# A graph layer and a mixture of experts in one kernel: logits from unnormalised tokens, and where the round's stores are awaited

## What is computed

```python
x = x + gnn(layernorm(x))          # 625 tokens x 512
x = x + ffn(layernorm(x))

# gnn: 16 relations' products H[r] = xn @ W_rel[r].T + b_rel[r], 10625 edges (both ways),
#      summed by target node, plus xn @ W_self.T + b_self, relu
# ffn: logits = xn @ router_w.T (16 experts), top 2, softmax over the two,
#      out = sum over the two experts of weight * (silu(xn @ gate) * (xn @ up)) @ down
#      gate, up: 512 x 1024, down: 1024 x 512 for each expert
```

## Time and profile before

| what | value |
|---|---|
| time, median of 3 runs | 737.27 us (736.48 to 740.19) |
| the profiled execution's own time | 733.35 us |
| its span, first to last instruction | 731.6 us |
| PE busy | 694.9 us |
| DVE busy | 625.8 us |
| ACT busy | 502.0 us |
| POOL busy | 309.9 us |

### The profile page before, as it was taken

The page is one execution under the profiler, slowest core; times in us unless marked ns, Lnnn a source line. Parts: engine busy times, 40 slices in busy tenths (PEclk is TensorE's granted clock), DMA queues, the critical chain, the costliest instruction groups (busy, mean ns, idle before and its releaser), DMA issues. The chain is left out here.

```text
span 731.6 us, 10688 instructions
## 1 busy us (share of the span) xinstructions
PE 694.9 (95%) x3210; PEld 542.9 (74%) x3210; DVE 625.8 (86%) x1289; ACT 502.0 (69%) x717; POOL 309.9 (42%) x279
## 2 busy tenths in 40 slices
PE   5899999999998999999997999999999999999993
PEld 4777766777676777777755788888888888888883
DVE  8889979998999677777775899999998999999990
ACT  3655476665675777777556498888877888888870
POOL 3000077851787677777771033332234333333201
PEclk9999999999999999999998899999999999999997
DMA  7347589884888889998767989999999999999932
GB/s 243 126 144 270 168 267 305 299 257 144 301 281 295 276 280 306 315 295 244 217 196 239 379 321 354 405 394 392 405 355 396 370 379 374 361 403 379 357 110 30
DMA packets 54436, 212.75 MB, mean 291 GB/s; under 512 B 9753, under 2 KB 10150, under 8 KB 39158
## 3 DMA queue, kind: packets, MB, share of 16 engines
q1 hardware_dynamic: 34998, 153.85, 55.9%
q0 software_dynamic: 19392, 58.35, 27.4%
HBM read 184.36 MB, written 27.80 MB: 290 GB/s over the span
## 5 line engine op out<-in xcount | busy, mean ns | idle before, releaser
L400 POOL DMA_INDIRECT rows_sb<-h_dram,row_of x190 | 212.5, 1119 | 165.3 <-DVE row_of L549 84.1
L559 DVE TENSOR_TENSOR rows_lo<-rows_sb,rows_hi 128x512 fp32r<-128x512 f32 x175 | 120.1, 686 | 43.5 <-ACT rows_hi L697 43.4
L830 PE MATMUL p_h<-g_hi_sb,xt_hi_whole 128*125 128x512 f32 x320 | 128.4, 401 | 0.3 <-DVE g_lo_sb L503 0.3
L831 PE MATMUL p_h<-g_lo_sb,xt_hi_whole 128*125 128x512 f32 x320 | 126.7, 396 | 0.0
L832 PE MATMUL p_h<-g_hi_sb,xt_lo_whole 128*125 128x512 f32 x320 | 126.5, 395 | 0.0
L697 ACT CAST rows_hi<-rows_sb 128x512 fp32r<-128x512 f32 x175 | 100.1, 619 | 25.5 <-DMA rows_sb<-h_dram,row_of 23.3
L682 ACT COPY h_whole<-p_h 125x512 f32<-125x512 f32 x80 | 46.9, 586 | 89.2 <-PE p_h L832 89.1
L1195 POOL DMA_INDIRECT tokens<-token_dram,rows_of_tokens x15 | 22.1, 1470 | 170.8 <-ACT rows_of_tokens L1484 131.5
L864 PE MATMUL p_sum<-rows_hi,seg_hot 128*125 128x512 f32 x175 | 73.6, 421 | 5.4 <-DVE rows_lo L559 4.5
L1248 DVE TENSOR_TENSOR u_lo_sb<-stage_up,u_hi_sb 128x2048 fp32r<-128x2048 f32 x34 | 76.4, 2288 | 1.0
L1248 DVE TENSOR_TENSOR d_lo_sb<-stage_down,d_hi_sb 128x2048 fp32r<-128x2048 f32 x32 | 71.8, 2286 | 3.0 <-ACT d_hi_sb L1469 2.9
(11 more groups left out here) (292 smaller groups left out, 1363.6 us busy)
## 6 DMA issues: line engine op xcount, KB each, us to landing
stage_up<-in_L_ffn_up_w SPq DMA_DIRECT2D x34, 1024.0 KB, 8.0
stage_gate<-in_L_ffn_gate_w SPq DMA_DIRECT2D x32, 1024.0 KB, 8.7
stage_down<-in_L_ffn_down_w SPq DMA_DIRECT2D x32, 1024.0 KB, 7.5
h_dram<-h_whole SPq DMA_DIRECT2D x80, 224.0 KB
stage_up<-in_L_gnn_W_rel SPq DMA_DIRECT2D x16, 1024.0 KB, 8.0
x_whole<-in_L_gnn_b_rel SPq DMA_DIRECT2D x16, 256.0 KB, 9.7
rows_sb<-h_dram,row_of POOLq DMA_INDIRECT x190, 5.1
h_dram<-h_whole SPq DMA_DIRECT2D x80, 26.0 KB
```

Source lines behind the costliest of these rows:

```text
L400: q.indirect_dma_start(rows_sb[:, b % ROWS], None, h_dram[0:1 + made(n) * TP], bass.IndirectOffsetOnAxis(ap=row_of[:, b:b + 1].bitcast(U32 ...
L559: v.tensor_tensor(rows_lo[:, b % PARTS], rows_sb[:, b % ROWS], rows_hi[:, b % PARTS].bitcast(F32), ALU.subtract).then_inc(part_lo, 1)
L830: m.matmul(o, xt_hi[:, dc, at], wt_hi_sb[:, 1 - j % 2, dc], start=(by_matmul and dc == 0), stop=False, skip_group_check=True)
L831: m.matmul(o, xt_hi[:, dc, at], wt_lo_sb[:, 1 - j % 2, dc], start=False, stop=False, skip_group_check=True)
```

## The change

- The router's weights are centred: at product 72 (ROUTER) four matmuls with an all-ones matrix sum `router_t` over the 512 features, and DVE subtracts the mean (`centre_router`, by product 73). The logits are then made of x2 instead of xn: PE's `turn` waits for x2 and not for the normalisation, and its logits are those of before times 1/rstd. The gap of the two best is multiplied by rstd before Exp.
- PE's turns and logits come one tile sooner in its list, and so do ACT's copies.
- The last tile is normalised, and split in parts, in the second block: ACT at its beginning, DVE's `last_low` between the two groups of one-hots.
- SP no longer waits for the up weights and the stores at the round's end. Those two semaphores are no longer cleared; whoever overwrites x2's memory or reads the up weights waits for them: SP before the loads of d (and in the next round before its first weights), POOL before its gathers, ACT before the high parts of u. The token rows' store waits for the last tile.
- In the second block `choose` is cut in `candidates` and the rest, and the early one-hots go ahead of most of it; x_low(0) goes ahead of `chosen` and of u's first low part. PE picks expert 1's first two tiles ahead of `turn_tokens(0)` and the rest behind it, ahead of the ranks, with one `keep_going` matmul in place of three. On ACT both picked_copy and x_high(0) go ahead of Exp and Silu.

```diff
@@ on_sync
+                sp.wait_ge(up_loaded, nth_round * 32 + 16)
+                sp.wait_ge(x2_stored, nth_round * (32 * T) + 16)
                 w_load(0)
...
                     sp.dma_start(out[t * TP + MAIN:(t + 1) * TP], x2[MAIN:TP, t]).then_inc(x2_stored, 16)
-                sp.wait_ge(up_loaded, 32)
-                sp.wait_ge(x2_stored, 32 * T)
@@ on_vector
+                def centre_router():
+                    dve.wait_ge(router_summed, 1)
+                    v.scalar_tensor_tensor(router_t[:], p_router.unsqueeze(1).to_broadcast([P, KC, NX]), -1 / D, router_t[:],
+                                           ALU.mult, ALU.add).then_inc(router_ready, 1)
...
+                    if i == ROUTER + 1:
+                        centre_router()
...
                     if t:
                         token_lows(t - 1)
-                token_lows(T - 1)
@@ on_scalar
                 for t in range(T):
-                    if t >= 2:
-                        x2_copy(t - 2)
-                    if t == T - 1:
+                    if t:
                         x2_copy(t - 1)
-                    root(t)
-                    normal2(t)
-                    high2(t)
                     if t == T - 1:
                         x2_copy(t)
+                    root(t)
+                    if t < T - 1:
+                        normal2(t)
+                        high2(t)
                     carry_out(t)
+                act.wait_ge(scale2_ready, T)
@@ on_tensor
                 def turn(t):
-                    pe.wait_ge(ln2_ready, t + 1)
+                    pe.wait_ge(x2_ready, t + 1)
...
-                        i = m.transpose(p_h[:, t % 2, dc * TP:(dc + 1) * TP], xn[:, t, dc * P:(dc + 1) * P], ident[0:TP, 0:TP])
+                        i = m.transpose(p_h[:, t % 2, dc * TP:(dc + 1) * TP], x2[:, t, dc * P:(dc + 1) * P], ident[0:TP, 0:TP])
...
+                    if i == ROUTER:
+                        pe.wait_ge(small_loaded, 16)
+                        pe.wait_ge(rows_ready, 2)
+                        for dc in range(KC):
+                            r = m.matmul(p_router, ones[:], router_t[:, dc], start=(dc == 0), stop=(dc == KC - 1))
+                        r.then_inc(router_summed, 1)
...
                 for t in range(T):
                     for k in range(last_in_tile):
                         last_message(last_span + t * last_in_tile + k)
+                    if t:
+                        turn(t - 1)
                     if t >= 2:
-                        turn(t - 2)
-                    if t >= 3:
-                        token_logits(t - 3)
-                turn(T - 2)
-                token_logits(T - 3)
+                        token_logits(t - 2)
+                turn(T - 1)
                 token_logits(T - 2)
-                turn(T - 1)
                 token_logits(T - 1)
@@ first block, SP
+                    sp.sem_inc(up_loaded, 16)
+                    sp.sem_inc(x2_stored, 16)
                     sp.dma_start(edge[:], edges).then_inc(edge_loaded, 16)
@@ second block, SP and POOL
                     load("g", 1, 0)
                     load("g", 1, 1)
+                    sp.wait_ge(last_hi_ready, 1)
...
+                    sp.wait_ge(x2_stored, sp.snap(rounds_of(sp), min_val=1, max_val=ROUNDS) * (32 * T) + 16)
                     load("d", 0, 0)
...
+                    pool.wait_ge(x2_stored, pool.snap(rounds_of(pool), min_val=1, max_val=ROUNDS) * (32 * T) + 16)
                     pool.wait_ge(ln2_stored, 32)
@@ second block, DVE
+                    def last_low():
+                        dve.wait_ge(last_hi_ready, 1)
+                        v.tensor_tensor(xn_lo[:, T - 1], xn[:, T - 1], xn_hi[:, T - 1].bitcast(F32), ALU.subtract).then_inc(last_lo_ready, 1)
...
                     def chosen():
-                        v.tensor_tensor(mask[:, 0:T], hot[:, 0], hot[:, 1], ALU.add).then_inc(mask_ready, 1)
-                        v.tensor_tensor(gap[:], best[:, 1], best[:, 0], ALU.subtract).then_inc(gap_ready, 1)
+                        link("dve", dve, v.tensor_tensor(gap[:], best[:, 1], best[:, 0], ALU.subtract))
+                        v.tensor_tensor(gap[:], gap[:], rstd[:], ALU.mult).then_inc(gap_ready, 1)
...
                     early_masks()
+                    candidates(0)
+                    early_places()
+                    early_hots(0)
+                    last_low()
+                    early_hots(1)
                     choose(0)
-                    early_hots()
+                    candidates(1)
                     choose(1)
+                    v.tensor_tensor(mask[:, 0:T], hot[:, 0], hot[:, 1], ALU.add).then_inc(mask_ready, 1)
+                    x_low(0)
                     chosen()
                     low("u", 0, 0)
-                    x_low(0)
                     places()
@@ second block, ACT
                     act.sem_inc(split_hi["g"], 2)
+                    t = T - 1
+                    s.activation(xn[:, t], x2[:, t], ACT.Identity, bias=shift[:, t:t + 1], scale=rstd[:, t:t + 1]).then_inc(last_ln_ready, 1)
+                    act.wait_ge(last_ln_ready, 1)
+                    s.copy(xn_hi[:, t], xn[:, t]).then_inc(last_hi_ready, 1)
+                    n = act.snap(rounds_of(act), min_val=1, max_val=ROUNDS)
+                    act.wait_ge(x2_stored, n * (32 * T) + 16)
+                    act.wait_ge(up_loaded, n * 32 + 16)
                     high("u", 0, 0)
                     high("u", 0, 1)
+                    picked_copy(0)
+                    x_high(0)
+                    picked_copy(1)
                     act.wait_ge(gap_ready, 1)
                     s.activation(gap[:], gap[:], ACT.Exp).then_inc(exp_ready, 1)
...
                     s.activation(idle[:], gap[:], ACT.Silu)
-                    picked_copy(0)
-                    x_high(0)
-                    picked_copy(1)
                     x_high(1)
@@ second block, PE
-                    keep_going(3)
-                    pick_tokens(0)
+                    keep_going(1)
+                    pick_tokens(0, range(T))
+                    pick_tokens(1, range(0, 2))
+                    turn_tokens(0)
+                    pick_tokens(1, range(2, T))
                     pe.wait_ge(mask_ready, 1)
...
-                    turn_tokens(0)
-                    pick_tokens(1)
                     pe.wait_ge(xt_lo_ready, 1)
```

More of the change, by code:

```diff
@@ L43 @@
 LAG, START, PACE = 3, 22, 3.0
-LAST_HOTS = 56
+LAST_HOTS, ROUTER = 56, 72
 LOW, BIASES = 32, 2 * R + 1
@@ L119, in build @@
         gathered = [sem(f"gathered{i}") for i in range(ROWS)]
+        up_loaded, x2_stored = sem("up_loaded"), sem("x2_stored")
         steps, pool_steps = sem("steps"), sem("pool_steps")
         edge_consts, route_consts, spare_cleared = sem("edge_consts"), sem("route_consts"), sem("spare_cleared")
-        small_loaded, gate_loaded, x2_stored = sem("small_loaded"), sem("gate_loaded"), sem("x2_stored")
+        small_loaded, gate_loaded = sem("small_loaded"), sem("gate_loaded")
+        router_summed, router_ready = sem("router_summed"), sem("router_ready")
         bias_hi, bias_ready, self_ready = sem("bias_hi"), sem("bias_ready"), sem("self_ready")
@@ L249, in build @@
             p_logits = p_list[0:TP, 0:T * NX].rearrange("p (t e) -> p t e", t=T)
+            p_router = p_list[:, 256:256 + NX]
             p_ranks = p_sum[:, 0:3]
@@ L304, in turned, with on_sync @@
                 return p_sum[:, 3 + t % 2, 0:KC * TP].rearrange("p (c n) -> p c n", c=KC)
-            def on_sync(sp):
+            def on_sync(sp, nth_round):
                 def w_load(j):
@@ L932, in on_tensor @@
                             self_product(t)
-                pe.wait_ge(small_loaded, 16)
+                pe.wait_ge(router_ready, 1)
                 pe.wait_ge(round_counted, 1)
@@ L992, in _ @@
                     def _(sp):
-                        on_sync(sp)
+                        on_sync(sp, nth_round)
                     @block.gpsimd
@@ L1288, in early_hots, with candidates @@
                         link("dve", dve, v.scalar_tensor_tensor(early_place[:], p_early.rearrange("p (t e) -> p t e", t=T), 1.0, early_mask[:], ALU.add, ALU.mult))
-                        for e in range(2):
-                            for t in range(T):
-                                i = v.tensor_scalar(early_hot[e][:, t], slot_iota[:], 1.0, early_place[:, t, e:e + 1], ALU.add, ALU.is_equal)
-                                i.then_inc(early_hot_ready, 1)
-                    def choose(c):
+                    def early_hots(e):
+                        for t in range(T):
+                            i = v.tensor_scalar(early_hot[e][:, t], slot_iota[:], 1.0, early_place[:, t, e:e + 1], ALU.add, ALU.is_equal)
+                            i.then_inc(early_hot_ready, 1)
+                    def last_low():
+                        dve.wait_ge(last_hi_ready, 1)
```

(12 more changed lines are left out.)

5 lines of the change are left out of this document (3 added, 2 removed).

## The result

The changed kernel took 734.8 us (median of 20 runs, 728.16 to 739.66), the kernel before 737.95 on the same chip (20 runs, 734.91 to 741.38). The ratio is 0.9953 with a 95% interval of 0.9934 to 0.9972, so 3.5 us were gained, between 2.1 and 4.9. Its profiled execution took 732.14 us, its span is 730.4.

What follows compares the result with a forecast made beforehand. PE, busy 95%, was taken as the bound, with SP's wait for stores setting the round's boundary. Terms -4.15 + 0.55 + 0.1 - 0.35 = -3.85 us took 737.27 to 733.4 us; range 732.0 to 736.5.

Steps and rivals of the forecast that it cites:

- round's end, x2 to B: Graph layer's end: without SP's wait for stores, DVE arrives last at 395.6, not SP at 399.74; block begins 4.15 us earlier.
- router, in the product loop: PE's product loop: four new 16-column matmuls cost 0.55 us after a gap takes some; bounds 0 and 0.95.
- SP at the start, to the first product: Round's start: two semaphore increments before SP's first load cost 0.1 us, between 0 and 0.2.
- second block to the gate product: Second block up to expert 1's gate product: of some 2.4 us PE wins by reordering, 0.35 us remain.
- The wait moved to ACT: Second block's begin: ACT waits 1.1 us for stores landing at 400.4, holding u's high parts and all of expert 0.
- rival of stores delayed by loads: Round's end: gate-weight loads share the DMA engines, stores land 1 to 2 us later; gain 1.8 to 2.8, chance 0.23.
- ACT's 407.6 decides, by a little: Before x_low(0): ACT's u parts end at 407.6, PE's picks at 407.4, so ACT sets x_low(0) at 409.56.
- the low level at the block's begin and a rise 5 us into it: PE's clock: low at the second block's begin, rising 5 us in; a rise 2 us later costs about 1 us.
- A stall of about 2 us shows: Before expert 1's gate product: PE ready at 422.3, product can start at 424.3 behind DVE's first g low part.
- The block does begin earlier: Opposing rival: round's end waits on something hidden behind SP, so no earlier block; 737.4 us, chance 0.04.
- +4.6 us: Round's end rival: stores land behind loads and token rows, ACT begins u at 409; 741.9 us, chance 0.06.
- If PE entered at 2.4 GHz: Second block's begin: clock high, DVE decides instead of PE or ACT, worth at most 0.9 us; more gain's chance 0.12.

Runs made afterwards that it cites:

- base: The changed kernel with the second block's wait thresholds for stores and up weights written as constants for one round; 735.27 us against 737.67 for before, 0.9961.
- second profile of before: The unchanged kernel before, profiled again beside three experiments; 736.63 us, x2 to turns 39.35 us against 38.75 in its first profile.
- loads behind: The base with the two loads of expert 1's gate weights put behind the wait for the stores; 764.89 us, 1.0004, on a chip where before takes 764.7.
- old order: The base with the second block's work in the order of before, the last tile still normalised in it; 734.84 us, 0.9966 of before.
- slots late, end filler: The base with expert 1's slots work behind its gate product, plus four wide matmuls behind the last logits at the round's end; 737.7 us, 0.9993 of before.
- slots late, split: The base with slots work behind expert 1's gate product, turn_tokens(2) amid down(0), x_low(2) behind expert 2's first g low part; 738.57 us, 0.9992.
- the slots late: The base with slot_hots, PE's slots matmuls and ACT's copies of them moved behind expert 1's gate product; 737.63 us, 1.0013 of before.
- both fillers: The base with seven matmuls without a reader ahead of expert 1's gate product and four behind the last tile's logits; 736.28 us, 0.9961 of before.

## Why the prediction was right, and where it was off

Gains have a minus. The measured terms come from single profiles.

| term | predicted | measured |
|---|---|---|
| round's end, x2 to B | -4.15 | -4.27 (9.61 to 5.34), base -4.45 to -5.04 |
| router, in the product loop | +0.55 | +0.53 or +0.89 |
| SP at the start, to the first product | +0.10 | +0.17, in eight others +0.34 to +0.37 |
| second block to the gate product | -0.35 | +0.70 (23.45 to 24.15) |
| clock behind the stall | not in the sum | +1.53 (5.69 to 7.22) |
| rest | 0 | -0.3 |
| sum | -3.85 | -1.7 by the profiles; -3.5 (-4.9 to -2.1) timed |

**The round's end was right in mechanism and, as far as single profiles go, in size.** SP's wait set the boundary: put back, it takes the whole gain (1.0006). The logits were the next in line: with the waits alone moved, 1.2 to 1.8 us come in the profile. The last arriver is DVE at 396.87, and the barrier takes 1.27 us from there, beside 1.49. The prediction's term held the later last tile too (0.3), so the measured one in its terms is a little smaller than it looks; all three of its terms ahead of B together said that B comes 3.5 us earlier, and it came 3.09 earlier (401.23 to 398.14), in executions whose last x2 varies by more than that.

**The router's place was right, its price in part luck.** The set showed where it was expected, at 317.84. The prediction took 0.55 because a late gather had left a gap there; the second profile of before has no gap, and against it the price is 0.89, near the upper bound. That it is on the path to the end was argued and no run shows it. At SP's start, the first load of the round is issued 0.42 us later (4.79 to 5.21) and the first product starts 0.17 us later (15.24 to 15.41); in eight other profiles with these two increments it starts at 15.6; why it does is open.

**The wait moved to ACT as predicted, but it was not the decider.** ACT waited 1.38 us for the stores (1.1 predicted). They landed at 400.95, not 400.4. The rival of stores delayed by loads is neither shown nor ruled out: 5.1, 5.3 and 6.0 us without a load behind them, 5.4 to 6.9 with loads, so the ranges overlap and the second lies 0.9 us higher on the mean. The Trainium skill, DMA: Bandwidth & Descriptors (Queues, rings and completion order), says that each engine consumes a ring in order; by that the loads would cost the stores nothing, and these numbers don't decide it. What the rival had wrong is the price: where the stores took longest, 6.9 us, ACT's u parts were still done 0.35 us before the picks, so a later landing cost no time in any profile here.

**The step that failed is "ACT's 407.6 decides, by a little", and with it "the low level at the block's begin and a rise 5 us into it".** The clock was not low at the block's begin; it fell 0.7 us into it and rose 7.5 us behind B (398.14 to 405.6), not 5: B came 3.1 us earlier and the rise only 0.6 (406.2 before). In the profiles of the base and of the kernels with fillers or another order in the block it rose 6.0 to 8.3 us behind B, with the wait put back 6.3, in the two of before 5.0 and 4.7. The low stretch around the boundary lasted 6.8 us in the changed kernel and 10.2 in before and in the base. What sets its place and length is not shown. So all ten picks ran at 1.2 GHz, ended at 405.36, B + 7.2 and not B + 6.2, and ACT took them at 405.39 while its own u parts were done at 404.67. x_low(0) began at B + 9.42; 8.36 was predicted, and the price that the prediction gave for a rise 2 us later was about 1 us, all of it on the path. The kernel with the loads behind the stores settles that ACT's wait is not the decider: it waits for nothing there and the stage is no shorter. What a rise at B + 5 would have given in the new order, no run shows. From x_low(0) to the gate product the count was right, 14.73 us beside 14.74. DVE's wait ahead of x_low(0) is 2.17 us, 0.9 was expected; the same late picks.

**The stall was right, its after-effect was missing.** "A stall of about 2 us shows": it is 1.83. What I took for only lost waiting time can have a second price, the fall of the clock behind it: 1.5 us, in four profiles (changed, base, loads behind, and the one without centring), against none in the one with the wait put back, where PE stands still as long and the clock holds (426 to 427, and on). With seven wide matmuls in the stall it held in both profiles. Nor is the fall bound to this place or to the length of the wait. At other places in the block it came behind waits of 2.0 (old order), 2.6 (slots late, end filler) and 1.9 us (slots late, split), and it stayed away behind 1.8 us in both profiles of before and behind 2.7 us with the slots late: seven falls behind eleven waits of 1.8 to 2.7 us. The Trainium skill, TensorE: Matmul & The Clock Gate (Part 1), says that the place of a transition varies between runs of one kernel; a fall that comes in some executions and not in others fits that, and no run here tests it.

**No other rival came true.** The block does begin earlier, and nothing like +4.6 us shows. "If PE entered at 2.4 GHz" came true in the changed kernel, and for 0.7 us only, so its gain did not come; nor did it with fillers. No later stall appeared in the changed kernel: the rest is 300.9 us beside 301.2.

**What stays open.** The stages of the two profiles make 38.75 to 36.71 and 301.2 to 300.9, with router and start added a gain of 1.7 us; the base against the second profile of before makes 1.8 with these two, and 1.2 with its own (0.89 and 0.35). The timed ratios say 2.1 to 4.9 and 0.9 to 4.8. So that the forecast of 3.85 came near the timed 3.5 is in part luck: two of its steps were too favourable, by 1.05 and 1.53 us, and nothing measured makes up for them. A profile shows one execution, and whether the clock falls behind the stall in each of the timed ones is not known: without it 1.5 us more would be won. That the clock differs between executions is on record: the base's fastest one (731.1 us) has a mean granted clock of 0.990, its slowest (739.5) 0.979. I could not show that this is the difference. Nor is a faster version shown: the kernel with both fillers has 0.9961, as the base.

## What to carry to other kernels

A wait ahead of a barrier is worth its distance to the next arriver, and no more: shorten that one in the same change, or most of the gain stays away (1.2 to 1.8 us here, and nothing that shows in the time). Do not carry the place of a clock's rise over from the kernel before: when the block began 3.1 us earlier, the low stretch did not move with it. Cost the first matmuls at 1.2 GHz until a row shows otherwise. A reordering that lets PE arrive before DVE buys a stall, and a stall can cost a second time through the clock, which fell behind seven of eleven waits here (1.5 us where its price was read); and before moving a small step later to fill it, look at what its result starts: here the list of rows, which starts all later gathers.

## What I had not expected of the hardware

- PE's clock fell to 1.2 GHz behind the wait of 1.8 us ahead of expert 1's gate product, for 3.4 us, in four profiles of five; with seven matmuls of 512 columns in that wait it stayed at 2.4 GHz, in two profiles. Elsewhere it held behind a wait of 2.7 us.
- Stores of 10 pieces landed 5.1 to 6.9 us behind the last issue, with the DMA engines full at it; in one execution, with the last tile's stores 2.9 us behind the others, in under 3.4 us.
- Four matmuls of 512 columns at the round's end did not shorten the low stretch across the barrier (10.2 us in one profile, 6.8 in the other).
